# A mixer's written-out list of work: another order of tiles, and bank waits counted from the list

## The reference

```
x = x + attention(layernorm(x))
x = x + ffn(layernorm(x))      # kind 1
x = x + hydra(layernorm(x))    # kind 2
x = x + ffn(layernorm(x))      # kind 3
```

## Time and profile before

| | us |
|---|---|
| median of 3 runs (lowest, highest) | 3110.08 (3106.48, 3111.67) |
| the profiled execution | 3110.4 |
| its span | 3108.7 |
| its granted TensorE clock, mean | 0.954 of 2.4 GHz |
| TensorE busy | 2869.6 |
| VectorE, GpSimd, ScalarE busy | 1697.3, 879.2, 837.6 |

### The profile page before, as it was taken

One profiled execution on the slowest core, in us unless ns is written; L12 is line 12 of the kernel. 1 busy time (PEld: TensorE's weight loads), 2 busy tenths in 40 slices (PEclk: granted clock), 3 DMA queues, 4 the chain that ended last, 5 costly groups with the idle time before them and its releaser, 6 DMA issues. The chain is left out here.

```text
span 3108.7 us, 41774 instructions
## 1 busy us (share of the span) xinstructions
PE 2869.6 (92%) x16704; PEld 2139.2 (69%) x16704; DVE 1697.3 (55%) x2976; ACT 837.6 (27%) x1485; POOL 879.2 (28%) x1379
## 2 busy tenths in 40 slices
PE   5889999999999999999998786999999999999988
PEld 4556767667676676676775545877777777777766
DVE  4564464553644545636444144666666666666654
ACT  2342242231422322314223012222222222222220
POOL 0112122121221221212212014434353535353521
PEclk9889999999999999999998868999999999999989
DMA  5665445444445554445354330010101010102011
GB/s 150 173 174 153 156 102 159 106 113 141 111 92 159 113 147 120 102 140 121 81 145 117 100 138 1 1 35 21 38 18 41 14 48 8 54 1 55 1 28 28
DMA packets 103619, 272.29 MB, mean 88 GB/s; under 512 B 12122, under 2 KB 23514, under 8 KB 101122
## 3 DMA queue, kind: packets, MB, share of 16 engines
q1 hardware_dynamic: 99488, 268.56, 31.8%
q10 hardware_dynamic: 3938, 1.06, 0.2%
HBM read 168.40 MB, written 50.33 MB: 70 GB/s over the span
## 5 line engine op out<-in xcount | busy, mean ns | idle before, releaser
L483 DVE TENSOR_REDUCE top<-ps_attn 128x1 f32<-128x512 f32 (+3 forms) x704 | 420.0, 619 | 353.1 <-PE ps_attn L648 353.0
L394 ACT ACTIVATE pt<-ps_attn 128x512 f32<-128x512 f32 (+1 forms) x704 | 382.6, 559 | 758.6 <-PE ps_attn L675 756.1
L1379 PE MATMUL ps_mixer<-m_w_hi,m_xt_hi 128*128 128x512 f32 x1024 | 416.3, 407 | 0.0
L334 POOL TENSOR_SCALAR_AFFINE_SELECT pt<-pt 128x512 f32<-128x512 f32 x256 | 166.5, 662 | 875.6 <-ACT pt L394 873.2
L1380 PE MATMUL ps_mixer<-m_w_hi,m_xt_lo 128*128 128x512 f32 x1024 | 401.7, 392 | 0.0
L1381 PE MATMUL ps_mixer<-m_w_lo,m_xt_hi 128*128 128x512 f32 x1024 | 401.4, 392 | 0.0
L645 PE MATMUL ps_attn<-k_stack,q_stack 96*128 96x512 f32 (+3 forms) x1024 | 310.1, 360 | 55.1 <-DVE top L483 48.6
L675 PE MATMUL ps_attn<-q_stack,k_stack 97*128 97x512 f32 (+3 forms) x1024 | 285.4, 338 | 9.6 <-DMA q_stack<-top_rows 8.5
L645 PEld LDWEIGHTS ps_attn<-k_stack,q_stack 96*128 96x128 f32 x1024 | 178.7, 193 | 147.7 <-DVE top L483 114.6
L1045 ACT CAST m_xt_hi<-ps_mixer 128x512 fp32r<-128x512 f32 x192 | 104.4, 589 | 629.5 <-PE ps_mixer L1374 629.2
L492 DVE RECIPROCAL att<-ps_attn 128x128 f32<-128x128 f32 x256 | 241.1, 944 | 18.1 <-PE ps_attn L683 18.1
(11 more groups left out here) (207 smaller groups left out, 4992.5 us busy)
## 6 DMA issues: line engine op xcount, KB each, us to landing
xr<-in_a_x SPq DMA_DIRECT2D x64, 512.0 KB, 7.0
q_stack<-q_hi SPq DMA_DIRECT2D x128, 256.0 KB, 5.6
wq_hi<-wq_split SPq DMA_DIRECT2D x56, 512.0 KB, 4.1
wq_lo<-wq_split SPq DMA_DIRECT2D x56, 512.0 KB, 5.2
q_stack<-q_lo SPq DMA_DIRECT2D x64, 256.0 KB, 6.8
wo_hi<-wo_split SPq DMA_DIRECT2D x8, 2048.0 KB, 8.9
wo_lo<-wo_split SPq DMA_DIRECT2D x8, 2048.0 KB, 13.2
x<-xr SPq DMA_DIRECT2D x32, 512.0 KB, 2.8
```

Of the source, the lines that this page charges most:

```text
L394: nc.scalar.activation(pt[k][:, heads[0]:heads[0] + len(heads), :].rearrange("p j t -> p (j t)"), ps[:, ST0 + n % 2, 0:width * len(heads)] ...
L483: nc.vector.tensor_reduce(out, ps[:, S0 + n % 2, 0:width * len(heads)].rearrange("p (j k) -> p j k", k=width), AX.X, ALU.max).then_inc(s_u ...
L1379: nc.tensor.matmul(out, a_hi, b_hi, start=first, stop=False)
```

## The change

The first 20 or so entries of the list stay. Behind them the two lists differ in these places:

- `moments (3,3)` stands ahead of `h_conv 0 1`, and turn (3,3) right behind `h_gates 0`; from `h_cb 0` on every gemm of kind 3 comes one place later beside the hydra, so that gemm (3,3) 1 stands behind `h_back 0` and turn (1,1), and gemm (1,0) 0 behind `h_in 1`.
- `h_weight 0` stands ahead of turn (1,0) and behind add (3,2) 0; add (3,2) 1 stands behind `h_sum 0`, where it stood ahead of `h_mix 0`.
- Kind 1 is finished before kind 2 of the next block begins: turn (1,3) stands ahead of turn (2,0) and (2,1). Behind `h_back 1` come, for TensorE: turn (2,0), gemm (1,3) 0, `h_out 1`, turn (2,1), gemm (1,3) 1, down (2,0), turn (2,2), up 0, turn (2,3), up 1, down (2,2), up 2, turn (3,0), up 3, gemm (3,0) 0. Before, they were: gemm (1,3) 1, `h_out 1`, turn (2,2), up 0, turn (2,3) and so on, with turn (2,0), turn (2,1) and down (2,0) earlier.
- The counts on which `gemm` and `down` wait come from the places in the list, not from the numbers of the tiles; `add_up` of tile t waits for `post` of its own tile, where tile 0 waited for that of tile 3.

```diff
--- before.py
+++ after.py
@@ -783,23 +783,23 @@
 
 
     ORDER = [
-        ("up", 0), ("add_up", 0), ("turn", (2, 3)), ("moments", (3, 0)), ("up", 1), ("add_up", 1), ("norm", (3, 0)), ("down", (2, 2)),
-        ("up", 2), ("add_up", 2), ("turn", (3, 0)), ("up", 3), ("moments", (3, 1)), ("add_up", 3), ("norm", (3, 1)),
-        ("gemm", (3, 0), 0), ("add", (3, 0), 0), ("turn", (3, 1)), ("h_in", 0), ("gemm", (3, 0), 1), ("h_conv", 0, 0),
-        ("moments", (3, 2)), ("add", (3, 0), 1), ("norm", (3, 2)), ("gemm", (3, 1), 0), ("turn", (3, 2)), ("h_conv", 0, 1),
-        ("gemm", (3, 1), 1), ("add", (3, 1), 0), ("moments", (3, 3)), ("h_gates", 0), ("norm", (3, 3)), ("add", (3, 1), 1),
-        ("gemm", (3, 2), 0), ("turn", (3, 3)), ("h_turn", 0), ("add", (3, 2), 0), ("moments", (1, 0)), ("gemm", (3, 2), 1),
-        ("norm", (1, 0)), ("h_cb", 0), ("turn", (1, 0)), ("h_weight", 0), ("add", (3, 2), 1), ("gemm", (3, 3), 0), ("h_mix", 0), ("h_norm", 0),
-        ("moments", (1, 1)), ("h_sum", 0), ("add", (3, 3), 0), ("norm", (1, 1)), ("gemm", (3, 3), 1), ("h_back", 0), ("turn", (1, 1)),
-        ("add", (3, 3), 1), ("h_scale", 0), ("gemm", (1, 0), 0), ("moments", (1, 2)), ("norm", (1, 2)), ("h_out", 0),
-        ("turn", (1, 2)), ("add", (1, 0), 0), ("h_in", 1),
-        ("gemm", (1, 0), 1), ("h_conv", 1, 0), ("add", (1, 0), 1), ("moments", (2, 0)), ("gemm", (1, 1), 0),
-        ("add", (1, 1), 0), ("norm", (2, 0)), ("h_conv", 1, 1), ("gemm", (1, 1), 1), ("turn", (2, 0)), ("add", (1, 1), 1),
-        ("moments", (2, 1)), ("h_gates", 1), ("norm", (2, 1)), ("gemm", (1, 2), 0), ("h_turn", 1), ("turn", (2, 1)),
-        ("moments", (1, 3)), ("add", (1, 2), 0), ("norm", (1, 3)), ("gemm", (1, 2), 1), ("turn", (1, 3)), ("add", (1, 2), 1), ("h_cb", 1),
-        ("down", (2, 0)), ("h_weight", 1), ("h_mix", 1), ("h_norm", 1), ("moments", (2, 2)), ("h_sum", 1),
-        ("gemm", (1, 3), 0), ("norm", (2, 2)), ("h_back", 1), ("add", (1, 3), 0), ("h_scale", 1), ("gemm", (1, 3), 1),
-        ("h_out", 1), ("turn", (2, 2)), ("add", (1, 3), 1), ("moments", (2, 3)), ("norm", (2, 3)),
+        ("up", 0), ("add_up", 0), ("turn", (2, 3)), ("moments", (3, 0)), ("up", 1), ("add_up", 1), ("norm", (3, 0)),
+        ("down", (2, 2)), ("up", 2), ("add_up", 2), ("turn", (3, 0)), ("up", 3), ("moments", (3, 1)), ("add_up", 3),
+        ("norm", (3, 1)), ("gemm", (3, 0), 0), ("add", (3, 0), 0), ("turn", (3, 1)), ("h_in", 0), ("gemm", (3, 0), 1),
+        ("h_conv", 0, 0), ("moments", (3, 2)), ("add", (3, 0), 1), ("norm", (3, 2)), ("gemm", (3, 1), 0), ("turn", (3, 2)),
+        ("moments", (3, 3)), ("h_conv", 0, 1), ("gemm", (3, 1), 1), ("norm", (3, 3)), ("add", (3, 1), 0), ("h_gates", 0),
+        ("add", (3, 1), 1), ("turn", (3, 3)), ("h_turn", 0), ("gemm", (3, 2), 0), ("moments", (1, 0)), ("h_cb", 0),
+        ("norm", (1, 0)), ("add", (3, 2), 0), ("h_weight", 0), ("turn", (1, 0)), ("gemm", (3, 2), 1), ("h_mix", 0),
+        ("h_norm", 0), ("moments", (1, 1)), ("h_sum", 0), ("add", (3, 2), 1), ("norm", (1, 1)), ("gemm", (3, 3), 0),
+        ("h_back", 0), ("turn", (1, 1)), ("add", (3, 3), 0), ("h_scale", 0), ("gemm", (3, 3), 1), ("moments", (1, 2)),
+        ("norm", (1, 2)), ("h_out", 0), ("turn", (1, 2)), ("add", (3, 3), 1), ("h_in", 1), ("gemm", (1, 0), 0),
+        ("h_conv", 1, 0), ("gemm", (1, 0), 1), ("add", (1, 0), 0), ("h_conv", 1, 1), ("add", (1, 0), 1), ("moments", (1, 3)),
+        ("gemm", (1, 1), 0), ("h_gates", 1), ("norm", (1, 3)), ("turn", (1, 3)), ("add", (1, 1), 0), ("h_turn", 1),
+        ("moments", (2, 0)), ("gemm", (1, 1), 1), ("norm", (2, 0)), ("h_cb", 1), ("add", (1, 1), 1), ("h_weight", 1),
+        ("gemm", (1, 2), 0), ("h_mix", 1), ("h_norm", 1), ("h_sum", 1), ("add", (1, 2), 0), ("moments", (2, 1)),
+        ("gemm", (1, 2), 1), ("norm", (2, 1)), ("add", (1, 2), 1), ("h_back", 1), ("h_scale", 1), ("turn", (2, 0)),
+        ("gemm", (1, 3), 0), ("moments", (2, 2)), ("h_out", 1), ("turn", (2, 1)), ("add", (1, 3), 0), ("norm", (2, 2)),
+        ("gemm", (1, 3), 1), ("down", (2, 0)), ("add", (1, 3), 1), ("moments", (2, 3)), ("norm", (2, 3)), ("turn", (2, 2)),
     ]
     Y0, XT0, DOWN, UP0 = 0, 2, 1, 5
 
@@ -911,6 +911,13 @@
         index = {key: e for e, key in enumerate(events)}
         kind2 = [e for e, (_, kind, _) in enumerate(events) if kind == 2]
         gemms = [e for e, (_, kind, _) in enumerate(events) if kind != 2]
+
+        downs_ahead, gemms_ahead = {}, {}
+        for name, i, what, *part in plan:
+            if name == "gemm" and part == [1]:
+                downs_ahead[index[(i, *what)]] = len(gemms_ahead)
+            elif name == "down":
+                gemms_ahead[index[(i, *what)]] = len(downs_ahead)
 
         def event(i, what):
             return index[(i, *what)]
@@ -1159,8 +1166,7 @@
                     nc.vector.tensor_tensor(half, ps[:, Y0 + h, :], half, ALU.add).then_inc(y_added, 1)
 
                 def add_up(i, t):
-                    if t == 0:
-                        dve.wait_ge(post_done, PIECES * (event(i, (2, TILES - 1)) + 1))
+                    dve.wait_ge(post_done, PIECES * (event(i, (2, t)) + 1))
                     for h in range(2):
                         dve.wait_ge(up_ready, 2 * (TILES * i + t) + h + 1)
                         half = xs[:, i % 2, t, h * HALF:(h + 1) * HALF]
@@ -1382,12 +1388,11 @@
 
                 def gemm(e, h):
                     g, s = gemms.index(e), e % 3
-                    downs = len([n for n in kind2 if n < e])
                     pe.wait_ge(xlo_done, 2 * (e + 1))
                     if g:
                         pe.wait_ge(y_added, 2 * (g - 1) + h + 1)
-                    if h == 1 and downs:
-                        pe.wait_ge(h_done, downs)
+                    if h == 1 and downs_ahead[e]:
+                        pe.wait_ge(h_done, 2 * downs_ahead[e])
                     cols = slice(h * HALF, (h + 1) * HALF)
                     for k in range(CH):
                         if g == 0 and h == 0:
@@ -1399,7 +1404,7 @@
                 def down(e):
                     n, cols = kind2.index(e), turned_pair(e)
                     pe.wait_ge(xlo_done, 2 * (e + 2))
-                    pe.wait_ge(y_added, 2 * len([g for g in gemms if g < e]))
+                    pe.wait_ge(y_added, 2 * gemms_ahead[e])
                     if n:
                         pe.wait_ge(h_done, n)
                     else:
```

## The result

| | before | after |
|---|---|---|
| median (lowest, highest), 4 runs each | 3108.28 (3106.39, 3111.67) | 3147.74 (3143.77, 3149.30) |
| ratio, 95% interval | | 1.0124 [1.0109, 1.0139] |
| span of the profiled execution | 3108.7 | 3147.6 |

What follows compares the result with a forecast made beforehand. TensorE, working 92% of the span, was taken as the bound. The terms -11.4 - 6.4 + 19.2 - 16.5 + 12.4 - 3.0 - 5.0 = -10.7 us, from a median of 3110.1, gave 3100, range 3087 to 3114.

Steps and rivals of the forecast that it cites:

- signs of being wrong: No DMA wait on VectorE; a turn over 152 or under 147 us; gemm (3,0) 0 of turn 1 after 2038.
- slower through the clock: Rival, chance 0.15: five places where TensorE stops or has light work replace one long rest; three half-clock stretches a turn, 3117.
- part 1: Start of a turn: 1.9 us less up to gemm (3,0) 0, with GpSimd deciding; -11.4 over six turns.
- Part 4: Half-clock stretches in the six steady turns: 1.25 a turn, costing 12.4 us (0 to 20) where 10 cost 16.5.
- Part 3: Turn (1,2): a later store delays its tile's reload; 3.2 us more (2.7 to 3.7), +19.2 over six turns.
- Part 2: At h_mix 0: mixing weights come earlier and the rest goes; 1.6 us less in four of six turns, -6.4.
- `h_cb 0` has 4 us to spare: Before h_cb 0: softplus comes later behind inverse root (3,3) on GpSimd, but 4 us of slack covers it.
- Part 5: Head, from the first turn (1,2) through h_in 0 to the steady turns: net 3.0 us less.
- Part 6: Tail, turn 7: the rest of 2.09 goes and h_in 1 gains 2.7 at full clock; 5.0 us less.
- The bank counts at nothing: Waits of gemm, down and add_up: the new counts were put at no cost.
- the reload arrives in time: Rival, chance 0.05: store and reload take under 8.4 us together, so turn (1,2)'s delay and its half-clock stretch vanish; 3071.
- The estimate of 6.4 us for the pair: Store and reload before turn (1,2), by the Trainium skill's DMA figures; the trace's 11.5 was used instead.

Runs made afterwards that it cites:

- e8: Old list up to h_in 1 with h_weight 0 ahead of turn (1,0), new list behind, down (2,0) moved behind turn (2,2): 3085.98, ratio to before 0.9925.
- e5: Changed kernel with moments (3,3) behind h_conv 0 1 (softplus first) and turn (3,3) behind h_turn 0: 3139.51, ratio to before 1.0102.
- e3: Changed kernel with moments, norm and turn of tile (1,2) behind h_conv 1 0, ahead of add (1,0) 0: 3119.90, ratio to before 1.0039.
- e6: Changed kernel with moments, norm and turn of tile (1,2) moved behind h_in 1 and add (1,0) 0: 3110.25, ratio to before 1.0000.
- e9: Against e8: turn (2,0) behind h_norm 1, turn (2,2) and down (2,0) ahead of moments (2,3): 3055.85, ratio to before 0.9829.
- e0: Changed kernel with the list of before, so only the wait counts in gemm, down and add_up are new: 3102.57, ratio to before 0.9981.
- e4: Changed kernel with add (3,2) 1 ahead of moments (1,1) instead of behind h_sum 0: 3131.53, ratio to before 1.0059.

## Why the prediction was wrong

The sign was wrong. Two of the prediction's own signs of being wrong came: a turn of 156.9 (over 152), and gemm (3,0) 0 of turn 1 at 2044.58 (later than 2038). The likeliest mechanism for it stood among the rivals with a chance of 0.15 (slower through the clock, 3117), but even that was 31 us short. In the six turns the forecast was -2.7 (the sum's parts 1 to 4: -11.4, -6.4, +19.2, -4.1), the trace has +37.3: 40 us. Three terms make 38 of it (26, 5.6 and 6.4), part 1 most of the rest:

- **Part 4, the clock, failed, by some 26 us.** I took 1.25 stretches a turn away from the start, with bounds of 0 and 2, by the likeness to the rest of 3.63 that was followed by one. The trace has 3.8 (23 in six turns): two or three about one rest of 4.0 to 5.05, and one or two at turn (1,0), behind `h_cb 0`. The mistake is in what was compared: behind the rest of before stood a transposition and then `up` and `down`; behind this one stand the transposition and `h_in 1`, light float32 products, and ahead of it `h_out`. 16 stretches have become 23 where 7.5 were forecast. That the place counts and not only the length, two runs show: rests of 3.76 or 3.77 before turn (3,0) have one stretch each (e8), while the shortest rest before turn (1,2) in e5, 3.58, has two. That the light stages are the reason is not shown; in e3 and e6 they run at full clock once the long rest and the transposition are away from them. For the seven stretches at turn (1,0) the forecast had a quarter of one a turn at most; why they come is open.
- **Part 3, the reload, had the right mechanism and too small a term.** The wait came in all six turns, on VectorE, before the moments, as described. It is 4.34 on average where 3.4 was assumed, outside the bound of 3.7: 5.6 us in six turns. The add ended 5.29 after the start of `h_mix 0` (5.35 assumed); the pair took 12.9 us where I took 11.6. I had counted to the last bytes and 0.1 more. Here the bytes end by about 2425.2, and the moments start at 2426.16. The trace of before could not show this end, as nothing waited for it.
- **Part 2 was right for `h_mix 0` and missed what it moved.** The 1.22 rest is gone. But "`h_cb 0` has 4 us to spare" looked at TensorE alone; behind softplus's readers in VectorE's own queue stand `x_low` (3,3) and moments (1,0). The rest of 1.28 before turn (1,0) occurs in five of six turns, 6.4 us. With softplus first, in e5, it is gone; e5 also moves turn (3,3) behind `h_turn 0`, and the two were not tried apart.
- **Part 1 was right in its mechanism and 0.5 us a turn too good.** Rests of 0.90, 0.76 and 1.74 against 1.05, 0.8 and 1.5, gemm (3,0) 0 at 32.9 after `h_back 1` against 32.35. e8 and e9 show the reason given, the chain on GpSimd: taking away the first two rests gives nothing, shortening the chain gives 27 us.
- **Part 5, the head, failed by 9.3 us**: 6.3 more instead of 3.0 less. The stretch from turn (1,2) to `h_in 0` is right (1851.99 to 1914.34 is 62.35; forecast 62.6). (66.35 less 62.6 is 3.75; the forecast's sum used 3.5.) Turn (1,2) starts 3.55 later, of which 2.6 lie before the mixer's first load, in the unchanged program. From `h_in 0` to gemm (3,0) 0 it takes 6.7 more where 0.5 more were forecast: `h_in 1` of turn 0 is at half clock, and turn (3,0) rests 2.97; both were not foreseen. The rest of the 6.7 was not taken apart.
- **Part 6, the tail, was right**: 4.7 less against 5.0. `H_out 0` has no rest, and the layer change is at full clock (this answers to the earlier trace rows):

```profile
3047.59 0.60 PE L1514 MATMUL ps_mixer<-m_c_ident,m_tok 128*128 128x128 f32 x4
3048.86 1.06 PE L1440 MATMUL ps_mixer<-m_p_wdt_t,m_feat 128*128 128x8 f32 x8 [0.67 <-ACT m_feat L1099]
```

- **The bank counts at nothing: right** in that they cost nothing (e0, which is 0.2% faster than before).

The rival "the reload arrives in time" did not come: the pair took 12.9 us where it needed under 8.4. The estimate of 6.4 us for the pair is half of that. The Trainium skill ("DMA: Bandwidth & Descriptors", Anatomy of one DMA) gives the two figures behind it for transfers issued through GpSimd; here SyncE issues them, so the estimate took them to a path that they were not given for.

In e8 one rest of 3.77 brought a half-speed stretch that three rests of 0.90, 0.76 and 1.74 did not bring. The Trainium skill ("TensorE: Matmul & The Clock Gate", HAM oscillation) says that the cost of a fallen clock is paid anew at each break; the loss through the clock points the same way, but in e8 it was the length of one break that decided, not the number of breaks.

## What to carry to other kernels

When an instruction is moved behind others, look for what its completion releases: here an add one stage later delays a store, a reload and the next tile, and the price is paid 13 us further on. Cost a new rest together with the clock that may fall about it, and take the price from a rest at the same place: three short rests were free of it where one of 3.8 us cost one stretch and one of 4.3 us, elsewhere in the turn, two or three. And where a chain on a second engine sets the pace, change the order on that engine: moving TensorE's own `down` gave nothing, letting GpSimd's `post` run ahead of a root that must wait, with turn (2,0) begun earlier, gave 27 us.

## What was not expected of the hardware

- The clock was down in e5 and in the kernel before while TensorE was busy for 6.8 us without a rest, and in the changed kernel it stayed down for 10.2 us about a rest of 4.58. Shorter rests in the same place (e4) brought 6.8 us of half clock twice, at 2.23 and 2.53, and none four times, at 1.57 to 2.43.
- VectorE instructions of 0.13 to 0.19 us take 0.67 to 0.70 beside GpSimd's `post`, three to five times as long; and one small GpSimd instruction (L1016, changed kernel, at 2386.06) takes 1.08 instead of 0.25 us beside VectorE's `norm`.
- A reload of 512 KB can be read some 1 us after its last bytes have moved.
- In the twelve profiled executions the mixer's first load is issued between 1834.0 and 1841.4 us, though the program ahead of it is the same in all: a difference of a few us at the head of one profile says nothing.
